# Half-width scans and fills, 23 instead of 20 products on VectorE, expert loads one phase earlier, and a third bank for the last image's tail

## What is computed

```python
# 1: a linear attention with a fixed 1024x1024 weight gamma
q, k, v = x @ Wq + bq, x @ Wk + bk, x @ Wv + bv
y = (gamma * (q @ k.T)) @ v @ Wo + bo
h = where(y >= 0, y, a * y)
# 2: a state-space block, 128 inner channels, 16 states
x_main, x_gate = split(h @ W_in + b_in)
xc = silu(x_main @ W_conv + b_conv)
B, C = split(xc @ W_bc + b_bc)
dt = softplus(xc @ W_dt + b_dt)
h_n[t] = exp(dt[t] * A[n]) * h_n[t-1] + dt[t] * B[n, t] * xc[t]     # n = 0..15
y[t] = sum_n C[n, t] * h_n[t]
h = layernorm(h + (y * silu(x_gate)) @ W_out + b_out)
# 3: experts, one of 16 per group of 64 tokens, plus a shared one, two layers
f = relu(h @ Wi.T + bi)
for l in (0, 1): f = relu(f @ (Ws[l] + Wr[l, e] + I) + biases)
out = layernorm(h + f @ Wo.T + bo)
```

## Time and profile before

| what | value |
|---|---|
| median of 3 timed runs | 374.9 us (374.68 to 375.24) |
| the profiled execution, its own time | 371.63 us |
| its span, first to last instruction | 369.8 us |
| TensorE busy | 292.9 us (79%) |
| VectorE busy | 253.4 us (69%) |
| GpSimd busy | 264.1 us (71%) |
| ScalarE busy | 172.0 us (47%) |
| mean granted clock of TensorE | 0.866 |
| DMA, mean | 232 GB/s |

### The profile page before, as it was taken

One profiled execution on the slowest core, in us unless ns is written; L12 is line 12 of the kernel. 1 busy time (PEld: TensorE's weight loads), 2 busy tenths in 40 slices (PEclk: granted clock), 3 DMA queues, 4 the chain that ended last, 5 costly groups with the idle time before them and its releaser, 6 DMA issues.

```text
span 369.8 us, 4241 instructions
## 1 busy us (share of the span) xinstructions
PE 292.9 (79%) x1418; PEld 168.5 (46%) x1418; DVE 253.4 (69%) x225; ACT 172.0 (47%) x205; POOL 264.1 (71%) x116
## 2 busy tenths in 40 slices
PE   8998678865777899878977998694377939879595
PEld 4423313332352434647333446473344639555583
DVE  2556598976679899769895987797686676610110
ACT  3006714247954436786724467936635433314003
POOL 1035069998899989899995998899999799800000
PEclk9999959995995999999988999889685786989559
DMA  7940597766788899969789799677899985223101
GB/s 252 422 191 0 196 301 242 278 225 231 246 291 276 290 282 324 284 232 314 236 279 277 225 315 300 199 285 249 303 296 289 327 310 199 90 57 100 44 0 28
DMA packets 42998, 85.87 MB, mean 232 GB/s; under 512 B 7904, under 2 KB 24800, under 8 KB 42720
## 3 DMA queue, kind: packets, MB, share of 16 engines
q1 hardware_dynamic: 42576, 84.43, 69.2%
q10 hardware_dynamic: 400, 1.17, 1.1%
HBM read 75.62 MB, written 1.57 MB: 209 GB/s over the span
## 4 chain that ended last, share of the span: by engine, by line
PE 31%; DVE 24%; ACT 13%; POOL 12%; issue 11%; SPq 4%; DMA 4%; DVEq 0%; POOLq 0%; ACTq 0%
DVE h L974 14%; POOL ub L853 7%; PE work L479 6%; DVE decay L962 5%; POOL hc L862 5%; PE acc_r L488 5%; PE acc_y L531 5%; DMA c_row<-bc_dram 3%; PE tail L599 3%; ACT decay L693 2%; DVE mixed L992 2%; SPq L357 2%; ACT decay L673 2%; PE work L599 2%; PE acc_r L412 1%
## 5 line engine op out<-in xcount | busy, mean ns | idle before, releaser
L862 POOL TENSOR_TENSOR hc<-h,c_row 128x1024 f32<-128x1024 f32 x64 | 153.6, 2400 | 23.3 <-DVE h L974 22.4
L974 DVE TENSOR_TENSOR_SCAN h<-decay,ub 128x1024 f32<-128x1024 f32 x44 | 100.7, 2289 | 27.1 <-ACT decay L673 13.5
L853 POOL TENSOR_TENSOR ub<-u,b_row 128x1024 f32<-128x1024 f32 x44 | 103.8, 2358 | 13.1 <-DMA b_row<-bc_dram 13.1
L673 ACT ACTIVATE decay<-delta,neg_a 128x1024 f32<-128x1024 f32 x44 | 49.3, 1120 | 84.8 <-DVE h L974 84.8
L531 PEld LDWEIGHTS acc_y<-pack,hc 128*128 128x128 f32 x512 | 63.4, 154 | 44.7 <-issue 30.2
L531 PE MATMUL acc_y<-pack,hc 128*128 128x128 f32 x512 | 76.7, 298 | 5.8 <-POOL hc L862 5.8
L479 PE MATMUL work<-q,kT 64*128 64x512 f32 x112 | 37.3, 745 | 15.4 <-DVE mixed L992 10.2
L974 DVE TENSOR_TENSOR_SCAN h<-decay_own,decay 128x1024 f32<-128x1024 f32 x20 | 45.7, 2286 | 0.7
L992 DVE TENSOR_TENSOR mixed<-gam,work 128x512 f32<-128x512 f32 x56 | 35.6, 676 | 7.2 <-PE work L479 6.5
L488 PE MATMUL acc_r<-mixed,v_sb 128*64 128x512 f32 x128 | 38.2, 679 | 0.9 <-DVE mixed L992 0.8
L599 PEld LDWEIGHTS tail<-f,group_w 128*128 128x128 f32 x224 | 34.1, 232 | 0.9
(11 more groups left out here) (143 smaller groups left out, 302.2 us busy)
## 6 DMA issues: line engine op xcount, KB each, us to landing
b_row<-bc_dram SPq DMA_DIRECT2D x64, 512.0 KB, 5.1
c_row<-bc_dram SPq DMA_DIRECT2D x64, 512.0 KB, 5.4
group_w<-expert_w SPq DMA_DIRECT2D x64, 128.0 KB, 3.9
gam<-gammaT SPq DMA_DIRECT2D x8, 512.0 KB, 10.6
expert_w<-routed_w SPq DMA_DIRECT2D x1, 2048.0 KB, 18.3
x_in<-xT SPq DMA_DIRECT2D x4, 256.0 KB, 8.2
out<-res SPq DMA_DIRECT2D x8, 128.0 KB, 3.3
pack<-packed ACTq DMA_DIRECT2D x1, 788.0 KB, 6.9
```

What stands on the lines that cost most here:

```text
L673: nc.scalar.activation(target, delta[:, b % 2, :], ACT.Exp, scale=neg_a[:, n:n + 1])\
L853: nc.gpsimd.tensor_tensor(ub[:, j % 3, :], u[:, b % 2, :], b_row[:, k % 3, :], ALU.mult)\
L862: nc.gpsimd.tensor_tensor(hc[:, k % 3, :], h[:, k % 3, :], c_row[:, k % 3, :], ALU.mult)\
L974: nc.vector.tensor_tensor_scan(h[:, k % 3, :], factor, term, 0.0, ALU.mult, ALU.add).then_inc(scan_done, 1)
```

## The change

- `fill_slot`, the scan and VectorE's product are cut into two halves of 512 tokens for states 7 to 15 of images 0 to 2 and all states of image 3 (`halved`); the second half-scan starts from the last column of the first, `h[:, k % 3, 511:512]`. `scan_done`, `decay_ready`, `u_copied` and `ub_own` count halves. The first half of a fill waits for the first half-scan alone.
- In image 3 VectorE makes the products of the eight even states, before of five states.
- The scan of state 0 of image 0 stands ahead of the head's first `mixed`.
- SyncE looks up the expert numbers in steps 4 to 11 of the image's own scan phase and issues four expert loads per step in steps 12 to 15 there.
- ROWS moves from LATE to EARLY in step 17 (all images).
- Image 3's tail uses three banks: `tail`, a bank of `work`, `acc_r`. Both residual matmuls are made ahead of their inputs' wait. y is copied out of PSUM half by ScalarE, half by VectorE. The matmuls of `keep_warm` go to `decay` and stand elsewhere.
- At the start `wvo` is made as soon as the constants are there, the values go to `acc_r` and are copied by ScalarE, the other folded weights follow; in image 0 the B and C rows are written out ahead of ScalarE's table load.

```diff
+VECTOR_STATES = [STATES * b + s for b in range(IMAGES)
+                 for s in ((0, 4, 8, 10, 14) if b < IMAGES - 1 else range(0, STATES, 2))]
-    (14, LATE): ((USE_OUT2, REST),), (15, LATE): ((USE_VAR2, WHOLE),), (17, LATE): ((USE_ROWS, WHOLE),),
+    (14, LATE): ((USE_OUT2, REST),), (15, LATE): ((USE_VAR2, WHOLE),), (17, EARLY): ((USE_ROWS, WHOLE),),
-WARM_AT = {2: 1, 4: 2, 5: 4, 7: 1, 12: 1, 14: 2, 15: 4}
+TAIL_FILL_ALONE = dict(TAIL_FILL)
+TAIL_FILL_ALONE[(1, LATE)] = ((USE_OUT1, RESIDUAL),)
+TAIL_FILL_ALONE[(3, LATE)] = ()
+TAIL_FILL_ALONE[(7, LATE)] = ((USE_F0 + 1, WHOLE), (USE_OUT2, RESIDUAL))
+TAIL_FILL_ALONE[(13, LATE)] = ()
+WARM_AT = {1: 2, 2: 1, 4: 2, 5: 4, 14: 2, 15: 4}
+        def halved(k):
+            return k >= STEPS * (IMAGES - 1) or k % STEPS >= TILES - 1
...
+                    if scanned(k) and 4 <= n < 12:
+                        for g in (2 * n - 8, 2 * n - 7):
+                            look_up_group(p, g)
+                    if scanned(k) and n >= 12:
+                        for g in range(4 * n - 48, 4 * n - 44):
+                            load_group(p, g)
-                        if m < 8:
-                            load_group(b, 2 * m)
-                            load_group(b, 2 * m + 1)
...
-                    if p == IMAGES and n < 2:
-                        pe.wait_ge(side_read, side_use(IMAGES - 1, SIDE_BC) + 1)
-                        keep_warm(acc_r, 4)
+                    if p == IMAGES and n == 1:
+                        pe.wait_ge(scan_done, 2 * STEPS * IMAGES)
+                        keep_warm(slot, 2)
...
+                in_halves = k > 0 and halved(k - 1)
+                for i, columns in enumerate((slice(0, HALF), slice(HALF, T)) if in_halves else (slice(0, T),)):
+                    if k:
+                        act.wait_ge(scan_done, 2 * k - 1 + i if in_halves else 2 * k)
+                    if on_vector(k):
+                        nc.scalar.activation(slot[:, columns], u[:, b % 2, columns], ACT.Copy)\
+                            .then_inc(u_copied, (columns.stop - columns.start) // HALF)
+                    else:
+                        decay_exp(k, slot, columns)
...
             def scan_step(k):
+                pieces = ((slice(0, HALF), 1), (slice(HALF, T), 2)) if halved(k) else ((slice(0, T), 2),)
+                for columns, wanted in pieces:
+                    if on_vector(k):
+                        drive(k, columns, wanted)
+                        factor, term = decay_own[:, columns], slot[:, columns]
...
+                    if columns.start:
+                        dve.wait_ge(scan_done, 2 * k + 1)
+                    carry = h[:, k % 3, HALF - 1:HALF] if columns.start else 0.0
+                    nc.vector.tensor_tensor_scan(h[:, k % 3, columns], factor, term, carry,
+                                                 ALU.mult, ALU.add).then_inc(scan_done, (columns.stop - columns.start) // HALF)
...
+                if b == ALONE and n == 1:
+                    dve.wait_ge(hc_used, STEPS * (b + 1))
+                    nc.vector.tensor_copy(y_t[:, HALF:T], acc_y[:, HALF:T]).then_inc(y_read2, 1)
...
+                    if k == 0:
+                        scan_step(k)
                     if head is not None and n < TILES:
                         weight_scores(head, n)
```

More of the change, by code:

```diff
@@ L38 @@
 EPS = 1e-5
-VECTOR_STATES = (0, 4, 8, 10, 14)
-GPSIMD_STATES = [s for s in range(STATES) if s not in VECTOR_STATES]
+VECTOR_STATES = [STATES * b + s for b in range(IMAGES)
+                 for s in ((0, 4, 8, 10, 14) if b < IMAGES - 1 else range(0, STATES, 2))]
+GPSIMD_STATES = [k for k in range(STATES * IMAGES) if k not in VECTOR_STATES]
 FIRST_WORK_USES, WORK_USES = 12, 22
@@ L53 @@
 TAIL_USES = 13
-TAIL_SETUP = 2
+TAIL_SETUP = 3
 EARLY, LATE = 0, 1
@@ L308, in tail_at @@
                 return tail[:, :], tail_full, tail_read, TAIL_SETUP + TAIL_USES * b + use
-            if use % 2 == 0:
-                return tail[:, :], tail_full, tail_read, TAIL_SETUP + TAIL_USES * ALONE + use // 2
-            return work[:, 0:HALF], other_full, other_read, use // 2
+            bank, order = BANK_ALONE[use]
+            if bank == 0:
+                return tail[:, :], tail_full, tail_read, TAIL_SETUP + TAIL_USES * ALONE + order
+            if bank == 1:
+                return work[:, 0:HALF], other_full, other_read, order
+            return acc_r[:, :], third_full, third_read, order
         def tail_filled(b, use):
@@ L401, in _ @@
             pe.wait_ge(s_pack, 16)
+            nc.tensor.matmul(tail[:, 0:D], const("wvb", D), const("wo_tok", D), start=True, stop=True)\
+                .then_inc(tail_full, 1)
             def folded_weights():
-                nc.tensor.matmul(tail[:, 0:D], const("wvb", D), const("wo_tok", D), start=True, stop=True)
+                pe.wait_ge(tail_read, 1)
                 nc.tensor.matmul(tail[:, 192:192 + INNER], const("w_main_t"), const("w_conv"), start=True, stop=True)
@@ L552, in residual @@
                 source = hT[:, b % 2, :] if use == USE_OUT1 else h1T[:, :]
+                if b >= ALONE and use == USE_OUT2:
+                    pe.wait_ge(ln_out, 2 * b + 1)
                 nc.tensor.matmul(tail_at(b, use)[0], const("centre"), source, start=True, stop=False,
@@ L556, in last_part @@
             def last_part(b, n, half_step):
-                for use, part in TAIL_FILL.get((n, half_step), ()):
+                for use, part in (TAIL_FILL if b < ALONE else TAIL_FILL_ALONE).get((n, half_step), ()):
                     bank = tail_at(b, use)[0]
@@ L647, in _ @@
                         if b == IMAGES - 1:
-                            keep_warm(acc_r, WARM_AT.get(m, 0))
+                            keep_warm(slot, WARM_AT.get(m, 0))
                     if head is not None and n == 9:
```

153 lines of the change are left out of this document (82 added, 71 removed).

## The result

The changed kernel takes 353.91 us (median of 4 runs, 353.24 to 354.43) against 374.79 us for the one before in the same comparison: a ratio of 0.9451, 95% interval 0.9415 to 0.9487. It is faster. The forecast was 350.8 us with a range of 343 to 359, so sign and range held and the forecast was 3.1 us too good. The profiled executions stand at 353.91 against 371.63 us, spans 352.1 against 369.8: 17.7 us, where the sum of the prediction said 24.1. The profiled execution of before lies 3.2 us under its median and the one of after on its own, so terms are compared on 17.7, the time as a whole on the medians.

What follows compares the result with a forecast made beforehand. GpSimd was taken to bound the scans, in a ring with VectorE and ScalarE, and one serial chain the end. Terms 2.3 + 3 + 1.3 + 4 + 13.5 = 24.1 us off the 374.9 us median gave 350.8 us, range 343 to 359.

Steps and rivals of the forecast that it cites:

- The end, 13.5: After the last scan: three pieces together save 13.5 us, or 8.6 if TensorE's clock falls all the same.
- (a) of the prediction: In the end: y's transposes start 7.2 us after the last scan instead of 7.54, 0.3 us gained.
- (b): In the end: the residual matmul between gate products and OUT1 is made ahead, 1.8 us gained.
- (c): In the end, layer 1 to the copy: no expert-weight wait and clock staying at 1.00, 11.4 us gained.
- Start, 2.3: Start of image 0: with the scan first, GpSimd's first product with C starts 2.3 us earlier; bounds 0 and 2.3.
- the head has eight steps to make it up: At the start: the reason given for taking the full 2.3 us although the head's `mixed` comes later.
- Halves in states 7 to 15, 3: Images 0 to 2: earlier fills save GpSimd 3 us, bounds 0 and 8; each cut pair costs VectorE 0.15 us.
- ROWS early, 1.3: Image 2: the copy of y starts about 1.2 us sooner, shortening GpSimd's wait; 1.3 us gained, bounds 0 and 3.
- Image 3, 4: Image 3: three products leave GpSimd; 56.8 us plus 5.3 of layer waits against 65.9, gain 4, bounds 0 and 8.
- Rival B: Image 3 gains nothing: VectorE and TensorE become its bound and it keeps 65.9 us; 354.8 us total, chance 0.12.
- Expert loads moved, 0: Steps 12 to 15: extra loads may delay B and C rows in images 0 to 2, but buffers cover it; nothing.
- Rival D: Second half-scans, reading the carry from SBUF, block GpSimd's products like u: 41 us lost, 392 us total, chance 0.04.

Runs made afterwards that it cites:

- f: The kernel before with only the change's early expert look-ups and four expert loads a step in steps 12 to 15: 361.64 us, ratio 0.9664.
- p: l with ROWS back in LATE for image 2 alone: 349.94 us, ratio 0.9386.
- j: The changed kernel with the scan of state 0 of image 0 behind the head's first `mixed` pair again: 351.36 us, ratio 0.9407.
- l: The changed kernel with the edits of i, j and g together: 350.9 us, ratio 0.939.
- m: l with two unused warming matmuls on TensorE in each of steps 1 to 15 of image 3's scan: 352.11 us, ratio 0.9421.
- d: The kernel before with every count of the scan, fill, product and decay semaphores doubled, nothing cut or moved: 376.69 us, ratio 1.0072.
- a: The changed kernel with halves in image 3 alone, whole scans, fills and products in images 0 to 2: 357.79 us, ratio 0.9592.
- o: The changed kernel with ROWS made in LATE again for all images: 354.2 us, ratio 0.9485.
- b: The changed kernel with five VectorE products in image 3 instead of eight, still in halves: 355.22 us, ratio 0.9506.
- g: The changed kernel with the expert loads of images 0 to 2 in steps 0 to 3 of the next phase: 352.73 us, ratio 0.9424.
- i: The changed kernel with first halves counted on semaphores of their own, so all increments are 1: 352.98 us, ratio 0.9444.

## Why the prediction was right, and where it was wrong

- **The end, 13.5: right, measured 14.2.** f shows 12.8 of it from the loads alone. (a) of the prediction, 0.3 us before the transposes, was short: they start at 324.34 - 317.67 = 6.67 us after the last scan where 7.2 was worked out, and p shows another 1.1 us there, the price of ROWS ahead of the last `acc_y`, which the working had put into its 7.2 without a number of its own. (b), 1.8, measured 11.30 - 9.62 = 1.7, and (c), 11.4, measured 21.44 - 9.74 = 11.7, with the clock at 1.00.
- **Start, 2.3: wrong in sign.** The step that failed is "the head has eight steps to make it up". TensorE stands 5.44 us for the late `mixed`, VectorE then 2.26 us for TensorE's scores, and the next scan stands in VectorE's order behind it. j shows a loss of 1.6 us by stretches and 2.5 by medians. A second step failed the other way: the folded weights and the values in `acc_r` were costed at nothing, but in j, l, m and p, with the scan late as before, the first product is at 46.07 to 46.19, at least 1.7 us ahead of 47.91. (The profile of before is early here: d and f, with the same work up to this product, have it at 49.05 and 49.65.) Together the start gave about 0.2 at the second product with C. That the first came at 49 as forecast was therefore no proof of the term.
- **Halves in states 7 to 15, 3: right, 3.9 to 5.3** (a). The price of a pair was mis-sized: 0.35 us, near the upper bound of 0.4, and not 0.15. It was taken from overlapped products, and a second half-scan waits for the first, whose last column it reads (78.82 behind an end at 78.68). The Trainium skill (VectorE: DVE Perf Modes, "The TRN2 errata") gives a fixed cost that makes, as an estimate, 0.16 us a split; the products agree (0.67 to 0.70 us for 512 columns, 1.23 for 1024, 0.13 more), the scans do not.
- **ROWS early, 1.3: the mechanism was right.** GpSimd's wait in image 2 fell from 4.28 to 2.06 us and is back at 4.75 in o. By the median it brings 0.3 to 0.4 us, inside the interval; 1.0 is given back in the end.
- **Image 3, 4: wrong, 0.35.** Rival B came true, which had 0.12. The working had VectorE's load (eight pairs near 7.0 us; busy 54.55 / 8 = 6.8) and its wait for the expert layers (5.3; measured 5.0) right. The step that failed is "The eight pairs give 56.8 us against 65.9, if nobody waits for TensorE", which takes the pairs to run at the load of the fuller engine: besides the 5.0, VectorE waited 3.7 us for ScalarE's copies of u and 2.6 us at first half-scans. Two engines 83% full that hand work to each other in turn do not reach their own load. b shows that moving the three products hardly matters with the halves in place, and m that more clock with more matmuls does not help. No run has eight products and whole scans in image 3, so it is open whether the 16 x 0.35 = 5.6 us that the cuts cost VectorE there (an estimate from the pair above) ate what the products freed. Which link of the ring of VectorE, ScalarE, GpSimd and TensorE gives most is not settled; a fill tile with a second buffer would tell, and was not tried.
- **Expert loads moved, 0: not contradicted.** g finds 1.1 us, inside the intervals.
- **A term that was missing:** the increments of 2, which put a separate wait instruction ahead of each instruction that adds them. No term of the prediction named this. d shows 3.4 us in the kernel before; in the changed one i shows 0.8 us, unproved in size.
- **Rival D, products shut out by second half-scans: refuted.** The carry from SBUF does not count as u does. In the changed kernel 46 of GpSimd's products overlap a second half-scan, and none takes over 2.38 us. GpSimd's products with C have a mean of 2402 ns over the program, 2400 before, and the only stretched ones are the three beside u = dt * xc, both inputs in SBUF, 3.25 us each; the first:

```profile
104.87 3.25 POOL L907 TENSOR_TENSOR hc<-h,c_row 128x1024 f32<-128x1024 f32 x1 [0.56 <-DVE h L1026]
```

Of the 6.4 us by which the profiled sum fell short (24.1 against 17.7), image 3 makes 3.65 and the start 2.1; the end (0.7) and the halves (1.2 by stretches) gave more than promised. That leaves 2.5 us, in which ROWS, the separate waits, the small waits for B and C rows and the spread of a single profile lie; the runs do not divide it further. That the total held is in part luck: the end brought 14.2 of the 17.7 us, and the terms on the scans, 10.6 in the sum, brought 3.5. Their misses fit into the range because it was wide enough for rival B.

## What to carry to other kernels

The wait to remove is the one at the end of a serial chain: moving the last loads one phase earlier gave 11.6 to 12.5 us, and most finer edits to the stretch where three engines wait in a ring gave single microseconds. When an instruction is moved ahead of another on one engine, follow the overtaken one: here its consumer's consumer was the next thing in the same queue. And when a semaphore has to count finer events, give them a semaphore of their own rather than raise the old one by 2: here every instruction that added 2 lost the wait that it could carry itself.
